# Delta-rule kernel: the 32x32 blocks and their inverses cross DRAM in quarters, one DMA each

## The chip, the cores and the metric

One core of a Trainium2 chip runs the whole kernel. The metric is the device time of one execution in microseconds (us); the median of the runs is compared.

## The reference, cut to what matters

The block takes x (4 x 256 x 256, float32), normalises it, and adds to x two branches: a gated delta-rule attention with 16 key heads and 32 value heads of width 128, and a mixture of 8 experts with a shared one. The change touches the attention branch only. Its core, per sequence and value head:

```python
def step(St, inp):
    q_t, k_t, v_t, g_t, b_t = inp
    St = St * jnp.exp(g_t)[..., None, None]
    v_old = jnp.einsum('bhk,bhkv->bhv', k_t, St)
    delta = (v_t - v_old) * b_t[..., None]
    St = St + k_t[..., None] * delta[:, :, None, :]
    o = jnp.einsum('bhk,bhkv->bhv', q_t, St)
    return (St, o)
```

The kernel doesn't scan. For a chunk of 128 tokens the recurrence is a triangular system: with N the decayed, negated products of the keys among themselves, the deltas are (I - N)^-1 applied to the values. So for every chunk a unit triangular 128x128 matrix is inverted.

## The kernel before, in words

A first stage (to about 240 us) does the norm, the routing and the experts. The change is in the second stage, a software pipeline over the 16 key heads; one pass of it is called a head here. Per head there are B x REP = 8 pairs of a sequence and a value head, and two chunks of 128 tokens each: NM = 16 matrices to invert.

**Making N.** ScalarE writes silu of the convolved k and q into kq (L1018). TensorE multiplies them in the items K0 to K3 (L1297, L1299), one for each sequence. VectorE scales the products by the decays into nm (L1160), 16 instructions a head, each adding 1 to nm_made. Of each nm row, w = 0 holds key with key and w = 1 key with query.

**Inverting.** Only the four 32x32 blocks on the diagonal of a matrix (the quarters q = 0 to 3) are inverted by elimination, on GpSimd. The SP queue moves them through DRAM, so that each of the 64 blocks has rows of its own on a partition:

- blocks_out (L878): SP waits for nm_made; for each q and chunk k one DMA writes 8 blocks to n_scratch (L885, 8 DMAs of 32 KB); then, with all landed, two DMAs read all blocks into halves[0] (L890). The upper 64 partitions work on the even rows of the inverses, the lower 64 on the odd ones.
- eliminate (L952): 31 steps of two instructions on GpSimd (L969, L972) and a turning copy (L975). Their semaphore is elim.
- blocks_back (L893): after the last step SP writes the inverse rows to r_scratch (L897, one DMA), and after the turning copy the turned ones to rt_scratch (L899, one DMA). With the latter landed it reads the turned blocks in six DMAs (L904: q = 0, 1, 2 by even and odd rows, semaphore turned_in) and the plain ones in eight into rf (L909: q = 0 to 3 by even and odd rows, into every second partition, semaphore back_in).

**Putting the inverse together.** TensorE and ScalarE do this in turns. LA1 (L1310) waits for all six turned transfers and multiplies blocks of N by turned inverses; ScalarE copies to p1 (L1062). LA2 (L1324) waits for all eight plain transfers. LB1 (L1337) and LB2 (L1345) do the same for the 64x64 blocks; then the values are solved (U1, N21, U2) and the outputs made (O).

**Order.** Each engine works through its own written list, ORDER for TensorE, ORDER_A for ScalarE, ORDER_V for VectorE, and waits at whatever item isn't ready. TensorE's has "... K2 OUT4 P7 P0 LA1 K3 LA2 P1 OUT5 LB1 OUT6 LB2 P2 U1_0 ...", ScalarE's "... Z3 LA1 S5 S6 E3 LA2 P7 P0 ...", VectorE's "... P6 D3 OUT4 K3 P7 ...". So K3, the last part of N for the next head, stands behind LA1 of this head on TensorE, and its decay factors (E3) behind LA1 on ScalarE. P and Z are projections (L1256 to L1258), OUT the output projection (L1395). SP's list for a head is: the weights, blocks_back of this head, blocks_out of the next one, its decays (L871), w_out (L876). GpSimd's is: the low part of the next projection weights (L949), then the elimination of the next head. P0 waits for that low part.

Of the kernel before, what the change touches and what calls it, by code (L numbers as in the profile page):

```python
# [20 lines left out]
F32 = mybir.dt.float32  # L21
# [3 lines left out]
ALU = mybir.AluOpType  # L25
ACT = mybir.ActivationFunctionType

P = 128
B, S, D = 4, 256, 256
# [29 lines left out]
def build(nc, x, w_heads, w_out, w_b, w_a, dt_bias, A_log, norm_w, router_w, w_up, w_down, out):  # L59

    n_dram = nc.dram_tensor("n_scratch", (4, 2, REP * B, C32, C32), F32).ap()
    r_dram = nc.dram_tensor("r_scratch", (2, 4, 2 * REP * B, C32 // 2, C32), F32).ap()
    rt_dram = nc.dram_tensor("rt_scratch", (2, 4, 2 * REP * B, C32, C32 // 2), F32).ap()
    eg_dram = nc.dram_tensor("eg_scratch", (HK, REP * B * EC), F32).ap()

    with ExitStack() as ctx:
        def sb(name, shape, dt=F32, where=ctx):
            return where.enter_context(nc.sbuf_tensor(name, shape, dt))
# [585 lines left out]
        with ExitStack() as c3:  # L654
# [18 lines left out]
            nm = [sb(f"nm{i}", [P, BH, 2, EC], F32, c3) for i in range(2)]  # L673
# [8 lines left out]
            t64 = halves[1][0:C64].rearrange("p (m t) -> p m t", t=C64)  # L682
# [4 lines left out]
            tc2 = p1  # L687
# [29 lines left out]
            back_in = sem("inverse_blocks_in", c3)  # L717
            rt_out = sem("turned_inverse_blocks_out", c3)
            turned_in = sem("turned_inverse_blocks_in", c3)
            a_full = sem("ra_full", c3)  # L720
# [142 lines left out]
            def _(sp):  # L863
# [14 lines left out]
                def blocks_out(n, par):  # L878

                    at_least(sp, nm_made, 16, n, 16)  # L880
                    for q in range(4):
                        first = C32 * q
                        cols = nm[par][first:first + C32].rearrange("p m w e -> p (m w e)").rearrange("p (m k s) -> p k m s", k=3, s=S)
                        for k in range(2):
                            sp.dma_start(n_dram[q, k].rearrange("m i x -> i m x"), cols[:, k, :, first:first + C32]  # L885
                                         ).then_inc(blocks_out_sem, 16)
                    at_least(sp, blocks_out_sem, 128, n, 128)
                    at_least(sp, rt_out, 16, n, 0)
                    for h in range(2):
                        sp.dma_start(halves[0][C64 * h:C64 * (h + 1)],  # L890
                                     n_dram.rearrange("q k m i x -> (q k m) (i x)")).then_inc(rb_in, 16)

                def blocks_back(n, it):  # L893
# [3 lines left out]
                    sp.dma_start(r_dram.rearrange("h q m i x -> (h q m) (i x)"), rows[:, 0:HR * C32]).then_inc(r_out, 16)  # L897
                    sp.wait_ge(elim, NELIM * n + NELIM)
                    sp.dma_start(rt_dram.rearrange("h q m c i -> (h q m) (c i)"), halves[0][:, 0:C32 * HR]).then_inc(rt_out, 16)  # L899
                    sp.wait_ge(rt_out, 16 * n + 16)  # L900
                    at_least(sp, a_full, 1, it.a_before("U2_1"), 0)
                    for q, tile, step in ((0, t64[0:C32], C32), (1, t64[C32:C64, :, HR:], C32), (2, tc2[C64:C64 + C32], HR)):
                        for h in range(2):
                            sp.dma_start(tile[:, :, h * step:h * step + HR], rt_dram[h, q].rearrange("m c i -> c m i")  # L904
                                         ).then_inc(turned_in, 16)
                    sp.wait_ge(r_out, 16 * n + 16)
                    for q in range(4):
                        for h in range(2):
                            sp.dma_start(rf[C32 * q + h:C32 * (q + 1):2, :, C32 * q:C32 * (q + 1)],  # L909
                                         r_dram[h, q].rearrange("m i x -> i m x")).then_inc(back_in, 16)  # L910
# [27 lines left out]
            def _(gp):  # L938
# [13 lines left out]
                def eliminate(n, it):  # L952
# [4 lines left out]
                    at_least(gp, r_out, 16, n, 0)  # L957
# [39 lines left out]
            def _(a):  # L997
# [15 lines left out]
                def silu(n, it, q):  # L1013
                    a.wait_ge(conv_step, 24 * n + 3 * (q + 1))
                    if q < 4:
                        blk, half = piece(q)
                        at_least(a, kk_full, B, n, 0)
                        a.activation(kq[:, 2 * half:2 * half + 2, blk, :], conv[q % 2][:], ACT.Silu).then_inc(silu_made, 1)  # L1018
# [12 lines left out]
                def run(it):  # L1031
                    b, odd, items = it.b, it.odd, it.items_a
                    n, par = b + 1, 1 - odd
                    for item in items:
# [29 lines left out]
                        elif item == "LA2":  # L1064
# [3 lines left out]
                            a.copy(t64[C32:C64].rearrange("p m (h j) -> p m h j", h=2)[:, :, :, 0:HR],  # L1068
                                   bank[C32:C64].rearrange("p m (i h) -> p m h i", h=2))
# [44 lines left out]
            def _(v):  # L1114
# [18 lines left out]
                def key_scales(n, it, par):  # L1133
# [5 lines left out]
                    v.tensor_scalar(sk[:].rearrange("p (b c) -> p b c", c=2), sums[:, :, 0, :], EPS_L2, None, ALU.add).then_inc(small, 1)  # L1139
                    v.tensor_scalar(sqe[par][:].rearrange("p (b c) -> p b c", c=2), sums[:, :, 1, :], EPS_L2, EPS_RMS * P,  # L1140
# [8 lines left out]
                def decayed(n, par, b_, it):  # L1149
# [5 lines left out]
                    for c, lo, hi, at in ((0, 0, S, P), (1, S, EC, 0)):  # L1155
                        w = hi - lo
                        bank = it.bank[f"K{b_}" + "ab"[c]][:, 0:2 * w].rearrange("p (w s) -> p w s", w=2)
                        for r in range(REP):
                            bh = b_ * REP + r
                            v.scalar_tensor_tensor(out=nm[par][:, bh, :, lo:hi], in0=bank, scalar=wneg[:, 2 * b_ + c, r:r + 1],  # L1160
# [75 lines left out]
            def _(te):  # L1236
# [36 lines left out]
                def across(par, m, first, size):  # L1273

                    at = S * (m // BH) + first + size
                    return nm[par][first:first + size, m % BH, 0, at:at + size]

                def run(it):
                    b, odd, items = it.b, it.odd, it.items_te
                    n, par = b + 1, 1 - odd  # L1280
                    for item in items:
# [11 lines left out]
                        elif k == "K":  # L1293
# [3 lines left out]
                            te.matmul(bank[:], kq[:, i, 0, 0:P], kq[:, i, :, :].rearrange("p w s -> p (w s)"), start=True, stop=True)  # L1297
                            bank = fill(it, f"K{i}b")
                            te.matmul(bank[:, 0:S].rearrange("p (w s) -> p w s", w=2), kq[:, i, 0, P:S], kq[:, i, :, P:S],  # L1299
# [10 lines left out]
                        elif item == "LA1":  # L1310
# [3 lines left out]
                            te.wait_ge(turned_in, 96 * b + 96)  # L1314
# [131 lines left out]
```

## Time and profile before

| | us |
|---|---|
| median of 3 runs | 1172.33 |
| lowest and highest | 1170.95, 1179.87 |
| the profiled execution, device time | 1175.13 |
| its span in the trace | 1173.2 |
| mean granted TensorE clock in it | 0.952 |

The span is the time from the first to the last instruction in the trace, 1.9 us less than the device time of the same execution. A view lists for each engine how long it was busy; the rows of the timeline give the start, the length, the line and the form of instructions, merged where they follow each other, and in square brackets how long the engine had been idle before and what ended it. SPq is the queue of SyncE; a row of it is the time in which it issued a DMA, not that in which the data moved.

### The profile page before, as it was taken

Reading aid. Unit: us, or ns where it says so; the run is one execution under the profiler, and the core shown is the slowest. Engines: PE = TensorE matmul, PEld = TensorE weight load, DVE = VectorE, ACT = ScalarE, POOL = GpSimd, SP = SyncE. Lnnn points to the kernel's source line nnn. Section 1 sums busy time; section 2 is a strip of 40 time slices with the busy share of each in tenths; the row PEclk is TensorE's granted clock in tenths of the full one; section 3 lists DMA queues with packets and bytes.
Section 4 is the critical chain, followed back from the end, with each engine's and each line's share of the span. In section 5 each row is a group of like instructions: output and inputs, shape, how many; then the busy total and the mean of one; then the engine's idle time right before and its main releaser. Section 6 shows DMA issues by size and latency. Waiting matters only on the chain.

```text
span 1173.2 us, 22375 instructions
## 1 busy us (share of the span) xinstructions
PE 1051.0 (90%) x8190; PEld 801.7 (68%) x8190; DVE 813.8 (69%) x1469; ACT 601.5 (51%) x1150; POOL 519.3 (44%) x1140
## 2 busy tenths in 40 slices
PE   3999999966689989998989889998999999988867
PEld 3786666645476767776777767676778777776756
DVE  4622222259849878897979887987888797968424
ACT  2521222234556747574746656574757474745523
POOL 2421000055745547283828364554728282835520
PEclk9999999988879999999989999998989898999979
DMA  9930110044131323324142413232332413231111
GB/s 331 365 124 19 45 46 28 23 157 127 29 115 36 117 45 109 69 84 115 57 100 59 128 31 121 38 115 44 109 69 83 115 56 98 61 102 33 39 35 45
DMA packets 155098, 103.18 MB, mean 88 GB/s; under 512 B 125168, under 2 KB 139120, under 8 KB 151664
## 3 DMA queue, kind: packets, MB, share of 16 engines
q1 hardware_dynamic: 153456, 97.56, 28.6%
q0 software_dynamic: 1536, 4.20, 1.1%
q8 instruction: 67, 1.10, 0.4%
q14 instruction: 39, 0.32, 0.1%
HBM read 79.77 MB, written 21.95 MB: 87 GB/s over the span
## 4 chain that ended last, share of the span: by engine, by line
PE 27%; POOL 20%; SPq 9%; DVE 8%; DMA 8%; issue 5%; ACT 2%; POOLq 0%; DVEq 0%; ACTq 0%
POOL rows L972 10%; POOL rows L969 9%; SPq L909 4%; PE pj L1256 3%; DVE nm L1160 3%; DMA halves<-n_scratch 3%; PE rg L1395 3%; PE pj L1257 3%; PE pj L1258 3%; SPq L885 3%; DVE conv L1122 3%; PE rg L1362 2%; PE rg L1378 2%; SPq L904 2%; DMA rf<-r_scratch 2%
## 5 line engine op out<-in xcount | busy, mean ns | idle before, releaser
L1122 DVE SCALAR_TENSOR_TENSOR conv<-pj,taps,conv 128x510 f32<-128x510 f32 (+2 forms) x384 | 283.9, 744 | 104.2 <-ACT conv L1010 94.6
L969 POOL TENSOR_TENSOR rows<-rows,halves 128x126 f32<-128x126 f32 (+22 forms) x496 | 187.8, 379 | 336.8 <-DMA halves<-n_scratch 299.2
L972 POOL TENSOR_TENSOR rows<-rows 128x126 f32<-128x126 f32 (+22 forms) x496 | 195.2, 393 | 38.9
L1256 PE MATMUL pj<-xhi,whi 128*128 128x512 f32 x384 | 182.0, 474 | 20.7 <-DVE conv L1122 13.5
L1257 PE MATMUL pj<-xlo,whi 128*128 128x512 f32 x384 | 159.1, 414 | 0.0
L1258 PE MATMUL pj<-xhi,wlo 128*128 128x512 f32 x384 | 158.9, 414 | 0.0
L1160 DVE SCALAR_TENSOR_TENSOR nm<-rg,wneg,eg 128x512 f32<-128x512 f32 (+1 forms) x256 | 138.1, 607 | 10.5 <-ACT eg L1053 6.6
L1395 PE MATMUL rg<-wo,gated 128*128 128x256 f32 x512 | 138.0, 402 | 0.1
L1256 PEld LDWEIGHTS pj<-xhi,whi 128*128 128x128 f32 x384 | 76.0, 198 | 53.4 <-issue 29.9
L1395 PEld LDWEIGHTS rg<-wo,gated 128*128 128x128 f32 x512 | 99.6, 200 | 18.1 <-issue 1.3
L1010 ACT ACTIVATE conv<-pj,taps 128x512 f32<-128x512 f32 x128 | 87.6, 694 | 46.3 <-PE pj L1258 42.9
L1131 DVE TENSOR_TENSOR_SCAN eg<-eg,start 128x256 f32<-128x256 f32 x128 | 94.0, 791 | 0.5
L1258 PEld LDWEIGHTS pj<-xhi,wlo 128*128 128x128 f32 x384 | 76.5, 199 | 18.6
L1257 PEld LDWEIGHTS pj<-xlo,whi 128*128 128x128 f32 x384 | 77.0, 201 | 13.0
L1226 DVE SCALAR_TENSOR_TENSOR acc<-rg,fr,acc 128x256 f32<-128x256 f32 x128 | 60.9, 476 | 29.5 <-PE rg L1395 29.0
L1378 PE MATMUL rg<-nm,zz 128*128 128x256 f32 x256 | 77.6, 385 | 1.9 <-ACT zz L1088 1.9
L1096 ACT ACTIVATE vn<-rg,ssk 128x128 f32<-128x128 f32 x256 | 73.1, 384 | 0.4 <-PE rg L1307 0.4
L1297 PE MATMUL rg<-kq 128*128 128x512 f32 x128 | 70.1, 630 | 0.0
L977 POOL MEMSET rf<- 128x2048 f32 x1 | 1.8, 1804 | 148.9 <-POOLq L200 148.9
L1204 DVE SCALAR_TENSOR_TENSOR gated<-rg,nwneg,zs 128x512 f32<-128x512 f32 x64 | 46.2, 746 | 30.7 <-ACT sq L1104 16.5
L1229 DVE SCALAR_TENSOR_TENSOR acc<-rg,fr,acc 128x256 f32<-128x256 f32 x128 | 61.9, 484 | 4.5
L1362 PEld LDWEIGHTS rg<-vn,rf 128*128 128x128 f32 x512 | 61.8, 192 | 3.9 <-ACT rf L1082 1.2
(197 smaller groups left out, 1948.3 us busy)
## 6 DMA issues: line engine op xcount, KB each, us to landing
eg<-eg_scratch SPq DMA_DIRECT2D x16, 1536.0 KB, 7.9
wraw<-w_heads SPq DMA_DIRECT2D x16, 776.0 KB, 4.6
w1a<-w_up SPq DMA_DIRECT2D x10, 1024.0 KB, 9.7
halves<-n_scratch SPq DMA_DIRECT2D x32, 256.0 KB, 3.8
w2a<-w_down SPq DMA_DIRECT2D x8, 512.0 KB, 12.5
wo<-w_out SPq DMA_DIRECT2D x16, 256.0 KB, 2.7
n_scratch<-nm SPq DMA_DIRECT2D x128, 32.0 KB, 1.7
r_scratch<-rows SPq DMA_DIRECT2D x16, 256.0 KB, 2.0
```

Source lines behind the costliest of these rows:

```text
L969: gp.tensor_tensor(tmp, rb[:, 0:r, t:t + 1].to_broadcast([P, r, w]), nb[:, t:t + 1, t + 1:].to_broadcast([P, r, w]), ALU.mult).then_inc(el ...
L972: gp.tensor_tensor(rb[:, 0:r, t + 1:], rb[:, 0:r, t + 1:], tmp, ALU.add).then_inc(elim, 1)
L1010: a.activation(conv[j % 2][:], it.pbank[item][:], ACT.Copy, scale=taps[par][:, piece(j)[0], KS - 1:KS]).then_inc(tap_made, 1)
L1122: v.scalar_tensor_tensor(out=y, in0=it.pbank[item][:, :, 0:S - s], scalar=taps[par][:, piece(j)[0], KS - 1 - s:KS - s], in1=y, op0=ALU.mul ...
L1131: v.tensor_tensor_scan(decay, decay, start[:, 0:S], 0.0, ALU.mult, ALU.add).then_inc(decay_made, 1)
L1160: v.scalar_tensor_tensor(out=nm[par][:, bh, :, lo:hi], in0=bank, scalar=wneg[:, 2 * b_ + c, r:r + 1], in1=eg[:, r, b_, at:at + w].unsqueez ...
L1256: te.matmul(bank, whi[par][w], xhi[:, k, cols], start=(k == 0), stop=False)
L1257: te.matmul(bank, whi[par][w], xlo[:, k, cols], start=False, stop=False)
L1258: ins = te.matmul(bank, wlo[par][w], xhi[:, k, cols], start=False, stop=(k == KD - 1))
L1362: ins = te.matmul(bank[:, q * P:(q + 1) * P], rf[:, m, :], vn[:, m, :], start=True, stop=True)
L1378: te.matmul(bank[:, r * S:(r + 1) * S], zz[:, s, :], nm[odd][:, s, 1, 0:S], start=True, stop=False)
L1395: ins = te.matmul(bank[:, r * D:(r + 1) * D], gated[:, r, t * P:(t + 1) * P], wo[:, r, :], start=True, stop=True)
```

## The change

N's layout and those of the three scratch tensors are changed so that a quarter q of all 16 matrices moves in one DMA.

- nm holds for each pair 768 columns: query-key of the first chunk row (0 to 255), key-key of it (NEAR = 256), query-key of the second chunk (SECOND = 512), key-key of it (FAR = 640). The diagonal blocks of all 16 matrices then lie 384 columns apart. To get this order kq holds q first and k second, and the matrices are numbered by pair and chunk (m = 2 * pair + chunk).
- n_scratch is written in 4 DMAs of 64 KB (8 of 32 KB before).
- r_scratch has rows in their natural order, so it is written in two DMAs, even rows and odd rows, each row of 128 bytes put 256 bytes behind the last (before: one DMA with 2 KB in one piece for each partition). rt_scratch is written in two DMAs, each partition's 2 KB still in one piece.
- The turned blocks are read in 3 DMAs (6 before), the plain ones in 4 (8 before), into all 32 partitions of a quarter.
- The order of reading is: turned 0, turned 2, plain 1, plain 3, turned 1, plain 2, plain 0. LA1 waits for the first two, LA2 for plain 1 and 3, LB1 for turned 1, LB2 for plain 2 and 0.
- The engines' lists are as they were. Matmuls, copies and VectorE instructions are the same in number and size; some read or write in another stride.

```diff
                     for q in range(4):
-                        first = C32 * q
-                        cols = nm[par][first:first + C32].rearrange("p m w e -> p (m w e)").rearrange("p (m k s) -> p k m s", k=3, s=S)
-                        for k in range(2):
-                            sp.dma_start(n_dram[q, k].rearrange("m i x -> i m x"), cols[:, k, :, first:first + C32]
-                                         ).then_inc(blocks_out_sem, 16)
-                    at_least(sp, blocks_out_sem, 128, n, 128)
-                    at_least(sp, rt_out, 16, n, 0)
+                        first = NEAR + C32 * q
+                        rows_of = nm[par][C32 * q:C32 * (q + 1)].rearrange("p b e -> p (b e)").rearrange("p (m s) -> p m s", s=EC)
+                        sp.dma_start(n_dram[q].rearrange("m i x -> i m x"), rows_of[:, :, first:first + C32]
+                                     ).then_inc(blocks_out_sem, 16)
+                    at_least(sp, blocks_out_sem, 64, n, 64)
+                    at_least(sp, rt_out, 32, n, 0)
...
                     sp.wait_ge(elim, NELIM * n + NELIM - 1)
-                    sp.dma_start(r_dram.rearrange("h q m i x -> (h q m) (i x)"), rows[:, 0:HR * C32]).then_inc(r_out, 16)
+                    for h in range(2):
+                        sp.dma_start(r_dram.rearrange("q m (i h) x -> h (q m) i x", h=2)[h],
+                                     rb[C64 * h:C64 * (h + 1)]).then_inc(r_out, 16)
                     sp.wait_ge(elim, NELIM * n + NELIM)
-                    sp.dma_start(rt_dram.rearrange("h q m c i -> (h q m) (c i)"), halves[0][:, 0:C32 * HR]).then_inc(rt_out, 16)
-                    sp.wait_ge(rt_out, 16 * n + 16)
+                    for h in range(2):
+                        sp.dma_start(rt_dram.rearrange("q h m c i -> h q m (c i)")[h],
+                                     halves[0][C64 * h:C64 * (h + 1), 0:C32 * HR]).then_inc(rt_out, 16)
+                    sp.wait_ge(rt_out, 32 * n + 32)
                     at_least(sp, a_full, 1, it.a_before("U2_1"), 0)
-                    for q, tile, step in ((0, t64[0:C32], C32), (1, t64[C32:C64, :, HR:], C32), (2, tc2[C64:C64 + C32], HR)):
-                        for h in range(2):
-                            sp.dma_start(tile[:, :, h * step:h * step + HR], rt_dram[h, q].rearrange("m c i -> c m i")
-                                         ).then_inc(turned_in, 16)
-                    sp.wait_ge(r_out, 16 * n + 16)
-                    for q in range(4):
-                        for h in range(2):
-                            sp.dma_start(rf[C32 * q + h:C32 * (q + 1):2, :, C32 * q:C32 * (q + 1)],
-                                         r_dram[h, q].rearrange("m i x -> i m x")).then_inc(back_in, 16)
+                    def turned_back(q, tile, landed):
+                        sp.dma_start(tile.rearrange("p h m i -> p (h m) i"), rt_dram[q].rearrange("h m c i -> c (h m) i")
+                                     ).then_inc(landed, 16)
+                    def rows_back(q, landed):
+                        sp.dma_start(rf[C32 * q:C32 * (q + 1), :, C32 * q:C32 * (q + 1)],
+                                     r_dram[q].rearrange("m i x -> i m x")).then_inc(landed, 16)
+                    turned_back(0, t64[0:C32, :, :, 0:HR], turned_in)
+                    turned_back(2, tc2, turned_in)
+                    sp.wait_ge(r_out, 32 * n + 32)
+                    rows_back(1, back_odd)
+                    rows_back(3, back_odd)
+                    turned_back(1, t64[C32:C64, :, :, HR:], turned_mid)
+                    rows_back(2, back_even)
+                    rows_back(0, back_even)
...
                         elif item == "LA1":
-                            te.wait_ge(turned_in, 96 * b + 96)
+                            te.wait_ge(turned_in, 32 * b + 32)
...
                         elif item == "LA2":
-                            te.wait_ge(back_in, 128 * b + 128)
+                            te.wait_ge(back_odd, 32 * b + 32)
...
                         elif item == "LB1":
+                            te.wait_ge(turned_mid, 16 * b + 16)
...
                         elif item == "LB2":
+                            te.wait_ge(back_even, 32 * b + 32)
```

## Rows read from the trace of the kernel before

**Rows 1.** the page, part 1: busy time, share of the span, instructions

```profile
PE 1051.0 (90%) x8190; PEld 801.7 (68%) x8190; DVE 813.8 (69%) x1469; ACT 601.5 (51%) x1150; POOL 519.3 (44%) x1140
```

**Rows 2.** PE waits, 420 to 1020 us: waiter, waited for, us, times, longest

```profile
PE rg L1330 <- DMA rf<-r_scratch: 26.3, 11, 3.4
PE rg L1319 <- issue: 6.0, 5, 1.3
```

**Rows 3.** stretches: length, busy us of each engine, PEclk, DMA share, GB/s

```profile
487.20:542.10 54.90, 49.38 (x456) 38.62 (x456) 46.81 (x82) 33.37 (x66) 29.49 (x68) 1.00 0.30 82
542.10:596.00 53.90, 50.70 (x456) 39.65 (x456) 44.45 (x78) 33.48 (x66) 29.62 (x68) 0.96 0.31 83
...
420.00:1020.00 600.00, 560.36 (x5013) 438.87 (x5012) 499.14 (x867) 364.50 (x722) 325.86 (x751) 0.96 0.30 82
```

**Rows 4.** timeline of the SP queue, first and last steady head, one head, tail

```profile
420.52 0.33 SPq L897 DMA_DIRECT2D r_scratch<-rows  x1
...
528.40 0.33 SPq L897 DMA_DIRECT2D r_scratch<-rows  x1
529.58 0.33 SPq L899 DMA_DIRECT2D rt_scratch<-halves  x1
531.60 1.91 SPq L904 DMA_DIRECT2D halves<-rt_scratch  x4
533.55 1.02 SPq L904 DMA_DIRECT2D p<-rt_scratch  x2
534.62 5.91 SPq L909 DMA_DIRECT2D rf<-r_scratch  x8
542.10 4.82 SPq L885 DMA_DIRECT2D n_scratch<-nm  x8
548.20 1.13 SPq L890 DMA_DIRECT2D halves<-n_scratch  x2
...
1019.65 0.33 SPq L897 DMA_DIRECT2D r_scratch<-rows  x1
...
1079.74 5.16 SPq L909 DMA_DIRECT2D rf<-r_scratch  x8
1084.94 5.00 SPq L885 DMA_DIRECT2D n_scratch<-nm  x8
```

**Rows 5.** timeline of PE: the first matmul of LA1 and of LA2

```profile
536.30 0.18 PE L1319 MATMUL rg<-halves,nm 32*32 32x32 f32 x1 [1.23 <-issue]
...
542.16 0.21 PE L1330 MATMUL rg<-rf,p 32*32 32x32 f32 x1 [3.17 <-DMA rf<-r_scratch]
...
1131.12 0.23 PE L1319 MATMUL rg<-halves,nm 32*32 32x32 f32 x1 [6.89 <-issue]
```

**Rows 6.** timeline of DVE: the last four nm instructions of two heads

```profile
539.88 2.19 DVE L1160 SCALAR_TENSOR_TENSOR nm<-rg,wneg,eg 128x512 f32<-128x512 f32 x4 [1.86 <-ACT eg L1053]
...
594.54 2.19 DVE L1160 SCALAR_TENSOR_TENSOR nm<-rg,wneg,eg 128x512 f32<-128x512 f32 x4
```

**Rows 7.** timeline of POOL: an elimination's first instruction, and the copy behind it

```profile
552.93 0.24 POOL L969 TENSOR_TENSOR rows<-rows,halves 128x31 f32<-128x31 f32 x1 [18.65 <-DMA halves<-n_scratch]
...
581.81 1.18 POOL L975 COPY halves<-rows 128x512 f32<-128x512 f32 x1
```

**Rows 8.** issues of SP by line: count, ns min/median/max, first and last start

```profile
L885 SPq DMA_DIRECT2D n_scratch<-nm x128: 308/451/1818, 273.4 to 1089.5; - x128
L904 SPq DMA_DIRECT2D halves<-rt_scratch x64: 303/488/1417, 316.3 to 1127.6; - x64
L909 SPq DMA_DIRECT2D rf<-r_scratch x128: 601/609/1952, 319.3 to 1134.9; - x128
L222 SPq DMA_DIRECT2D xs_scratch<-start x2: 641/6576/12510, 12.3 to 13.0; - x2
```

**Rows 9.** stretches, as rows 3: reading turned blocks, and writing n_scratch

```profile
642.00:644.00 2.00, 2.00 (x11) 1.66 (x10) 2.00 (x5) 0.00 (x0) 1.47 (x4) 1.00 0.66 62
275.00:277.00 2.00, 0.00 (x0) 0.00 (x0) 2.00 (x6) 0.00 (x0) 0.00 (x0) 1.00 0.44 66
```

More of the change, by code:

```diff
@@ L672, in build @@
             ssk = sb("ssk", [P, NT], F32, c3)
-            nm = [sb(f"nm{i}", [P, BH, 2, EC], F32, c3) for i in range(2)]
+            nm = [sb(f"nm{i}", [P, BH, 2 * EC], F32, c3) for i in range(2)]
+            NEAR, SECOND, FAR = S, 2 * S, 2 * S + P
             halves = [sb(f"halves{i}", [P, NM * C64], F32, c3) for i in range(2)]
@@ L681, in build @@
             prod = rows[:, HR * C32:]
-            t64 = halves[1][0:C64].rearrange("p (m t) -> p m t", t=C64)
+            t64 = halves[1][0:C64].rearrange("p (h m j) -> p h m j", h=2, j=C32)
             rf = sb("rf", [P, NM, P], F32, c3)
@@ L1017, in silu @@
                         at_least(a, kk_full, B, n, 0)
[L1018 removed]
+                        a.activation(kq[:, 2 * half:2 * half + 2, 1 - blk, :], conv[q % 2][:], ACT.Silu).then_inc(silu_made, 1)
                     else:
@@ L1273, in across @@
                 def across(par, m, first, size):
-                    at = S * (m // BH) + first + size
-                    return nm[par][first:first + size, m % BH, 0, at:at + size]
+                    at = (FAR if m % 2 else NEAR) + first + size
+                    return nm[par][first:first + size, m // 2, at:at + size]
                 def run(it):
@@ L1296, in run @@
                             bank = fill(it, f"K{i}a")
-                            te.matmul(bank[:], kq[:, i, 0, 0:P], kq[:, i, :, :].rearrange("p w s -> p (w s)"), start=True, stop=True)
+                            te.matmul(bank[:], kq[:, i, 1, 0:P], kq[:, i, :, :].rearrange("p w s -> p (w s)"), start=True, stop=True)
                             bank = fill(it, f"K{i}b")
-                            te.matmul(bank[:, 0:S].rearrange("p (w s) -> p w s", w=2), kq[:, i, 0, P:S], kq[:, i, :, P:S],
+                            te.matmul(bank[:, 0:S].rearrange("p (w s) -> p w s", w=2), kq[:, i, 1, P:S], kq[:, i, :, P:S],
                                       start=True, stop=True).then_inc(kk_full, 1)
@@ L1360, in run @@
                             for q in range(4):
-                                m = c * BH + 4 * i + q
-                                ins = te.matmul(bank[:, q * P:(q + 1) * P], rf[:, m, :], vn[:, m, :], start=True, stop=True)
+                                m = 4 * i + q
+                                ins = te.matmul(bank[:, q * P:(q + 1) * P], rf[:, 2 * m + c, :], vn[:, c * BH + m, :], start=True, stop=True)
                             ins.then_inc(a_full, 1)
@@ L1369, in run @@
                                 s = 4 * i + q
-                                ins = te.matmul(bank[:, q * P:(q + 1) * P], nm[odd][:, s, 0, P:S], zz[:, s, :], start=True, stop=True)
+                                ins = te.matmul(bank[:, q * P:(q + 1) * P], nm[odd][:, s, NEAR + P:NEAR + S], zz[:, s, :], start=True, stop=True)
                             ins.then_inc(v_full, 1)
@@ L1377, in run @@
                                 s = i * REP + r
-                                te.matmul(bank[:, r * S:(r + 1) * S], zz[:, s, :], nm[odd][:, s, 1, 0:S], start=True, stop=False)
-                                ins = te.matmul(bank[:, r * S + P:(r + 1) * S], zz[:, BH + s, :], nm[odd][:, s, 1, S:EC],
+                                te.matmul(bank[:, r * S:(r + 1) * S], zz[:, s, :], nm[odd][:, s, 0:S], start=True, stop=False)
+                                ins = te.matmul(bank[:, r * S + P:(r + 1) * S], zz[:, BH + s, :], nm[odd][:, s, SECOND:FAR],
                                                 start=False, stop=True)
```

35 lines of the change are left out of this document (17 added, 18 removed).

## The prediction

> **What bounds the kernel now.** I read the page's busy times first. TensorE is busy 90% of the span and no other engine over 69% [rows 1], but an average doesn't say what stands in its way, so next come the steady heads, those that begin with the write of the inverse rows at 420.52 and at 1019.65 us [rows 4]: 11 heads in 599.13 us, 54.47 us each. In that stretch TensorE is busy 560.36 of 600 us at a mean granted clock of 0.96 [rows 3], which is 50.9 us a head; 3.6 us a head it is idle. Its waits name the cause: 26.3 us in 11 waits of LA2 for the plain blocks, 6.0 us in 5 at LA1 [rows 2]. After such a wait the clock is low for a while: the head from one LA2 to the next with 49.38 us of work ran at clock 1.00; the next, with the same 456 matmuls, took 50.70 at 0.96 [rows 3]. So all in all the missing blocks cost TensorE 2.4 + 0.55 us of idle time and about 1.5 us of slow clock (50.9 - 49.4).
>
> Then the SP queue, to see why they are late. Call the issue of the inverse rows (528.40) t = 0. The turned ones go at 1.18, have landed at 3.20, their six reads are issued until 6.17, the eight plain ones until 12.13 [rows 4]. LA1 starts at 7.90, LA2 at 13.76 [rows 5]. VectorE makes the last nm at 11.48 to 13.67, after a wait for ScalarE, which stood at LA1 [rows 6]; SP sends N at 13.70, starts reading it at 19.80 [rows 4], GpSimd starts the next elimination at 24.53 and the next copy behind it is at 53.41 [rows 7]. That is a closed ring:
>
> 7.9 (to LA1) + 5.8 (LA1 to nm) + 6.1 (N out) + 4.7 (N in) + 28.9 (elimination) = 53.4 us.
>
> So two rings bind by turns: this one at 53.4, and TensorE's own list, 49.4 of work plus its stalls and its slow clock. The average of both is the 54.5 seen. The step from LA1 to nm is longer when VectorE is behind: at 594.54 it makes the last nm with no idle time before it [rows 6].
>
> **The change, part by part.**
>
> *N out: 8 DMAs to 4.* Issuing 8 took 4.82 us here and 5.00 at 1084.94 [rows 4]; at the least and the median of one issue, with the gap of 0.04 between two, it would be 0.31 + 7 x 0.49 = 3.7 [rows 8]. The last needs about 1.3 more to land (548.20 less the end of the issues, 546.92). Four take 0.31 + 3 x 0.49 = 1.8 us. Each has twice the packets: 512 of 128 bytes, 32 for each of 16 DMA engines. What one costs: in 275 to 277 us only such writes ran, 0.44 x 16 x 2 us for 66 GB/s x 2 us / 128 B = 1031 packets, 13.7 ns each [rows 9]; 16 more for each engine are 0.2 us. Sum 1.8 + 1.5 = 3.3; I take 3.7, since issues get held up now too (4.82 for 3.7). It saves 2.4 us.
>
> *Does the issue grow with the packets?* No row shows a DMA of 1024 short pieces issued alone. L904's have 512 and take 488 ns, L885's 256 and take 451; the fill of xs_scratch, 2944 pieces of 512 bytes, was issued in 641 (its second stood 12.5 us in a full queue) [rows 8]. Bounds: 0.45 us if it doesn't grow, 1 us if it does as the pieces. The 641 ns row is nearest: I take 0.5.
>
> *Inverse rows and turned rows out: 1 + 1 DMAs to 2 + 2.* The second turned write is issued 0.35 us later. Ahead of it in the same queues are now 2048 packets of 128 bytes, 128 an engine x 13.7 = 1.75 us, instead of 128 packets of 2 KB. They start at about 0.9 and end near 2.7, where the turned ones would have started at 2.1: 0.6 us late at most. Together I take 0.6 (bounds 0.35 and 1.0). Turned blocks landed at 3.8. The Trainium skill, "DMA: Bandwidth & Descriptors", Rules for kernel authors, says two transfers to disjoint halves of the partitions serialise; by that the split costs just its issue, and the sum would be 0.25 less.
>
> *Turned blocks in: LA1 waits for two DMAs, not six.* Issues 0.3 + 0.5, the second starting at 0.35. A read of 64-byte pieces costs an engine 10.9 ns each (0.66 x 16 x 2 us for 62 GB/s x 2 us / 64 B = 1938) [rows 9], so 64 pieces are 0.7 us where 32 were 0.35. Now the last of six is issued at 534.08 and LA1 starts 2.2 later; new: 0.35 + 2.2 + 0.35 + 0.2 behind the first = 3.1 after the landing, against 4.7 now. LA1 at 3.8 + 3.1 = 6.9, say 7.0: 0.9 saved. P0 ahead of LA1 ends at 6.7 (LA1's start less its 1.23 us of idle time [rows 5]), so nothing else holds it.
>
> *Plain blocks in: LA2 waits for two.* They are the third and fourth in the queue: landed at 3.8 + 0.35 + 3 x 0.55 + 2.5 = 8.3. LA2 needs ScalarE's copy of LA1 and comes behind K3; with K3 done at about 539 less 0.9, LA2 starts near t = 9.7 without a wait. The 2.4 us idle time of a head goes, and most of the slow clock with it. The new waits of LB1 and LB2 (behind them stand OUT6, P2, U1) are for the fifth to seventh DMA, landed by about 3.8 + 0.35 + 6 x 0.55 + 2.4 = 9.9; LB1 comes behind P1 and OUT5, ten large matmuls after LA2: nothing. If that cover were gone, each us late would be one of TensorE's idle time.
>
> *Free otherwise:* swapped kq, nm's order, matmul operands in two runs of 32 columns: same sizes. SP is free at about 7.7 instead of 12.1, long before nm at 12.8. It counts at the edges: at 1084.94 it sent N in the breath after its last plain read [rows 4].
>
> **The sum.** Ring through GpSimd: 7.0 + 5.8 + 3.7 + 4.7 + 28.9 = 50.1. TensorE: 49.4 + 0.3 for its copy waits = 49.7. Two rings so close, with VectorE at 45.4 us a head (499.14 / 11), disturb each other: I add 0.7, 50.8 us a head, 3.7 less than now. Over 16 heads 58.6 (the first and last have the same steps, and the last LA1 wait of 6.89 us [rows 5] shrinks by all that came before): span 1173.2 - 59 = 1114. The profiled execution took 1.9 more than its span, 1175.1, and the median 2.8 less than that. So the median comes to 1114 - 0.9, rounded to 1114.
>
> **The rivals.**
>
> 1. *VectorE takes over.* It has 45.4 us of work in 50.8, conv, nm and acc in a fixed list. Where it had no idle time before nm [rows 6], an earlier LA1 gains nothing, and TensorE then waits for its PSUM banks. Against it: over 600 us TensorE's two longest waits are for the blocks, not for VectorE [rows 2]. If LA1 to nm becomes 7.3, the ring is 51.6, and with the 0.7, 52.3: 16 x 2.2 = 35 less, 1137.
> 2. *The issue grows with the pieces.* 1 us each: N out stays 6.1, the two turned reads take 2, turned out is 0.7 later: ring 53.2, 16 x 1.3 = 20 less, 1152. The 641 ns row speaks against it [rows 8].
> 3. *The short writes block the queue: slower.* Inverse rows go as 128-byte pieces, interleaved by two DMAs. If one costs 4 x 13.7 = 55 ns, an engine has 7 us of them, the turned rows land at 9, LA1 comes 5.2 later than I say, ring 55.3: 16 x 0.8 = 13 more, 1185. It decides from about 48 ns a packet on. Against it: n_scratch's are of that size [rows 9]. The same page of the Trainium skill, Specifications, says writes under 512 bytes are read, changed and written back. n_scratch's 13.7 ns contain that already, so by the page too it is my figure; only two DMAs meeting in one 512-byte line is not in the trace.
> 4. *No change:* the idle time moves to LA1 and the clock stays low: TensorE 50.9 + 3. Against it: the ring itself is shorter by parts that are on it.
>
> **Chances.** My forecast (1100 to 1126) 0.60, rival 1 0.16, rival 2 0.12, rival 3 0.06, rival 4 0.06. A measurement can tell 1% from no change, 12 us. Faster: 0.60 + 0.16 + most of 0.12 = 0.87; within 1%: 0.07; slower: 0.06. Low end: both rings at 49.7 with a full clock, 16 x 4.7 = 75 less, 1098. High end: rivals 1 and 2 up to 1150.
>
> **What would show it.** Right: SP's four N issues in under 2.2 us; LA2 without a wait; LA1 about 7 us after the first inverse-row DMA; 50 to 51 us a head; clock nearly 1.00. Wrong: issues of 1 us; turned rows landing after t = 4.8; VectorE at the head of TensorE's waits; LA2 gone from the list but LA1 in its place with 3 us a head.

## The result, and the profile after

| | before | changed |
|---|---|---|
| median of 20 runs, us | 1178.31 | 1180.25 |
| lowest to highest, us | 1170.95 to 1180.90 | 1177.38 to 1185.78 |
| ratio, 95% interval | | 1.0033 (1.002 to 1.0046) |
| span of the profiled execution, us | 1173.2 | 1179.9 |
| mean granted TensorE clock in it | 0.952 | 0.941 |

The forecast was 1114, 5% faster. The change made the kernel slower by 0.3%, a difference that its interval sets apart from none. Repeated in a later group of runs (change_again) it gave 1.002 (0.9999 to 1.0041).

The page of the changed kernel, part 1 (engine, busy us, share, instructions): TensorE is as busy as before [rows 1].

```profile
PE 1057.2 (90%) x8190; PEld 803.7 (68%) x8190; DVE 813.7 (69%) x1469; ACT 601.1 (51%) x1150; POOL 519.2 (44%) x1140
```

The waits of TensorE in it from 420 to 1020 us (waiter, waited for, us, times, longest), to be read against [rows 2]. LA2, which had stood 26.3 us, is gone from the list. LA1 has 37.7 us instead of 6.0.

```profile
PE rg L1330 <- issue: 37.7, 11, 4.8
PE rg L1363 <- issue: 3.7, 11, 0.3
PE pj L1268 <- issue: 3.4, 5, 1.3
```

The SP queue of the changed kernel for one head, against [rows 4]:

```profile
525.57 1.27 SPq L900 DMA_DIRECT2D r_scratch<-rows  x2
526.89 1.48 SPq L904 DMA_DIRECT2D rt_scratch<-halves  x2
532.76 0.33 SPq L910 DMA_DIRECT2D halves<-rt_scratch  x1
533.14 0.56 SPq L910 DMA_DIRECT2D p<-rt_scratch  x1
533.75 1.34 SPq L914 DMA_DIRECT2D rf<-r_scratch  x2
535.15 0.48 SPq L910 DMA_DIRECT2D halves<-rt_scratch  x1
535.67 1.12 SPq L914 DMA_DIRECT2D rf<-r_scratch  x2
541.89 1.91 SPq L887 DMA_DIRECT2D n_scratch<-nm  x4
546.32 1.15 SPq L892 DMA_DIRECT2D halves<-n_scratch  x2
```

The reads are as quick as forecast, seven in 4.03 us where fourteen took 8.93. But the first of them starts at t = 532.76 - 525.57 = 7.19, and before it did at 3.20: what SP waits for there is that the two DMAs of turned rows land. The stretches of the changed kernel show how they go (length, busy us of PE, PEld, DVE, ACT, POOL, PEclk, DMA share, GB/s):

```profile
528.00:529.00 1.00, 1.00 (x6) 0.90 (x5) 0.62 (x3) 0.69 (x1) 1.00 (x1) 1.00 0.77 117
529.00:530.00 1.00, 1.00 (x6) 0.77 (x5) 0.96 (x2) 0.00 (x0) 1.00 (x1) 1.00 0.24 58
530.00:531.00 1.00, 1.00 (x4) 0.54 (x3) 0.96 (x2) 0.59 (x2) 1.00 (x1) 1.00 0.25 84
531.00:532.00 1.00, 1.00 (x6) 0.83 (x5) 0.96 (x3) 0.58 (x2) 0.88 (x3) 1.00 0.23 88
```

To 529 the inverse rows go in short packets with most engines busy. Then come three microseconds at a DMA share (the mean busy share of the 16 DMA engines) of 0.23 to 0.25 and 58 to 88 GB/s: four of 16 engines' worth. The same turned rows in the kernel before, one stretch:

```profile
530.50:531.00 0.50, 0.50 (x5) 0.42 (x4) 0.50 (x2) 0.00 (x0) 0.50 (x1) 1.00 1.00 389
```

All 16 engines and 389 GB/s. The DMA packets in the traces (a packet is one contiguous piece, here of 2 KB) split the delay. From SP's issue of the first turned write to its seeing them landed it is 2.04 us on average in the kernel before and 6.05 in the changed one. The first packet starts 0.85 us after that issue before, 1.87 now; from the first packet to the end of the last it takes 0.82 us before, 3.75 now. So about 1.0 us is the later start and 2.9 the slow transfer.

A late LA1 then costs more than its idle time. In the changed kernel LA1 starts at 591.41 after 4.78 us of idle time; behind it the granted clock is half, 1.2 instead of 2.4 GHz, K3 comes late, and VectorE waits 6.35 us for it before the last nm. The first matmul, the stretch behind it, and VectorE's row:

```profile
591.41 0.23 PE L1330 MATMUL rg<-halves,nm 32*32 32x32 f32 x1 [4.78 <-issue]
```

```profile
591.40:596.00 4.60, 4.59 (x68) 2.97 (x68) 0.00 (x0) 2.23 (x5) 0.00 (x0) 0.50 0.30 41
```

```profile
596.23 2.19 DVE L1172 SCALAR_TENSOR_TENSOR nm<-rg,wneg,eg 128x512 f32<-128x512 f32 x4 [6.35 <-PE rg L1311]
```

The steps of the ring, each the mean over the 11 steady heads, taken from the timelines of SP, PE and POOL, in us from the first inverse-row DMA (in kernels that issue the turned rows first, from the last elimination step):

| kernel | turned rows landed | LA1 | LA2 | N sent | N read | elimination | a head |
|---|---|---|---|---|---|---|---|
| before | 3.24 | 8.51 | 13.69 | 14.60 | 20.56 | 25.66 | 54.47 |
| changed | 7.37 | 10.76 | 14.84 | 17.33 | 21.53 | 26.48 | 55.34 |
| rt16 | 4.57 | 8.57 | 11.35 | 14.51 | 18.51 | 23.45 | 52.30 |
| rt16_first | 4.25 | 8.13 | 11.28 | 14.20 | 18.44 | 23.56 | 52.54 |
| b_rt8 | 5.31 | 9.99 | 15.68 | 16.08 | 22.01 | 27.28 | 56.10 |
| b_rt4 | 6.38 | 11.05 | 16.78 | 17.33 | 23.44 | 28.70 | 57.60 |
| rt16_long | 4.21 | 7.58 | 10.71 | 13.56 | 17.68 | 22.70 | 51.60 |
| rt16_first_long | 4.25 | 7.61 | 10.68 | 13.55 | 17.78 | 22.84 | 51.84 |
| rt16_n8 | 4.77 | 8.43 | 11.85 | 14.68 | 20.53 | 25.44 | 54.43 |
| b_order | 3.33 | 7.31 | 10.72 | 13.48 | 18.94 | 24.12 | 53.03 |
| n4_alone | 3.22 | 8.93 | 13.96 | 15.04 | 19.39 | 24.44 | 53.34 |
| order_n4 | 3.24 | 7.21 | 10.34 | 13.30 | 17.64 | 22.46 | 51.34 |
| order_n4_short | 3.21 | 14.22 | 16.84 | 20.53 | 24.63 | 29.62 | 49.41 |

In the changed kernel N takes 4.2 us from sending to reading where it took 6.0, a gain of 1.8. The turned rows land 4.1 later; LA1 waits for two reads and not for six and so follows them by 3.4 instead of 5.3, which leaves it 2.25 later. LA1 to nm takes 6.6 for 6.1. Sum: 2.25 + 0.5 - 1.8, so 0.9 us a head longer.

### The profile page after: what moved, and what is told of

Its sections match the earlier page's. It is cut to its first block, busy times and chain, and to the rows that moved or that the text cites. A ratio compares the mean times of both kernels' runs of the same rounds, so it can differ in the third digit from the quotient of the medians.

```text
span 1179.9 us, 22231 instructions
## 1 busy us (share of the span) xinstructions
PE 1057.2 (90%) x8190; PEld 803.7 (68%) x8190; DVE 813.7 (69%) x1469; ACT 601.1 (51%) x1150; POOL 519.2 (44%) x1140
## 4 chain that ended last, share of the span: by engine, by line
PE 64%; issue 6%; DVE 4%; POOL 2%; ACT 1%; DMA 1%; SPq 0%; ACTq 0%; DVEq 0%
PE rg L1408 9%; PE pj L1268 8%; PE pj L1269 7%; PE pj L1270 7%; PE rg L1309 5%; PE rg L1375 5%; PE rg L1391 5%; PE rg L1383 3%; PE rg L1392 2%; PE rg L1311 2%; PE rg L1319 2%; PE rg L1363 2%; PE rg L1354 2%; PE rg L1301 1%; PE rg L1341 1%
## 5 line engine op out<-in xcount | busy, mean ns | idle before, releaser
L1268 PE MATMUL pj<-xhi,whi 128*128 128x512 f32 x384 | 179.2, 467 | 19.3 <-DVE conv L1135 12.6
L1269 PE MATMUL pj<-xlo,whi 128*128 128x512 f32 x384 | 156.0, 406 | 0.0
L1270 PE MATMUL pj<-xhi,wlo 128*128 128x512 f32 x384 | 155.3, 405 | 0.0
L1268 PEld LDWEIGHTS pj<-xhi,whi 128*128 128x128 f32 x384 | 74.8, 195 | 53.6 <-issue 32.6
L1238 DVE SCALAR_TENSOR_TENSOR acc<-rg,fr,acc 128x256 f32<-128x256 f32 x128 | 60.9, 476 | 29.6 <-PE rg L1408 29.0
L1076 ACT COPY p<-rg 128x512 f32<-128x512 f32 x16 | 9.8, 612 | 139.4 <-PE rg L1332 139.4
L1309 PE MATMUL rg<-kq 128*128 128x512 f32 x128 | 78.9, 702 | 0.0
L1330 PE MATMUL rg<-halves,nm 32*32 32x32 f32 x512 | 24.9, 215 | 58.9 <-issue 48.9
L1330 PEld LDWEIGHTS rg<-halves,nm 32*32 32x32 f32 x512 | 23.3, 131 | 65.2 <-issue 64.3
```

What stands on the lines that cost most here:

```text
L1268: te.matmul(bank, whi[par][w], xhi[:, k, cols], start=(k == 0), stop=False)
L1269: te.matmul(bank, whi[par][w], xlo[:, k, cols], start=False, stop=False)
L1270: ins = te.matmul(bank, wlo[par][w], xhi[:, k, cols], start=False, stop=(k == KD - 1))
L1309: te.matmul(bank[:], kq[:, i, 1, 0:P], kq[:, i, :, :].rearrange("p w s -> p (w s)"), start=True, stop=True)
```

## The experiments

The level of the times differs between groups of runs: the kernel before had a median of 1188.6 us beside the first group (chip 0: rt16, rt16_first, b_rt4, b_rt8), 1189.9 beside the second (chip 4: rt16_long, rt16_first_long, rt16_n8, b_order) and 1179.7 beside the third (chip 4 again: order_n4, n4_alone, change_again, order_n4_short). Ratios are each to the kernel before in the same group. Two theories stood after the result. **Engines:** the turned rows are written by 4 of the 16 DMA engines, because the outermost dimension on the DRAM side, the quarters, has size 4 and doesn't merge with the matrices (the halves lie between them). **Short writes:** the 2048 packets of 128 bytes ahead of them hold the queue, rival 3 of the prediction.

### The layout of the turned rows: rt16

```diff
-    rt_dram = nc.dram_tensor("rt_scratch", (4, 2, 2 * REP * B, C32, C32 // 2), F32).ap()
+    rt_dram = nc.dram_tensor("rt_scratch", (4, 2 * REP * B, 2, C32, C32 // 2), F32).ap()
...
-                        sp.dma_start(rt_dram.rearrange("q h m c i -> h q m (c i)")[h],
+                        sp.dma_start(rt_dram.rearrange("q m h c i -> h (q m) (c i)")[h],
```

> The changed kernel with one edit: rt_scratch is laid out as quarter, matrix, half, so that the outermost dimension of each of its two writes is 64 (quarter and matrix merge) and no longer 4; the turned tiles have matrix before half to match. Engine theory (a DMA runs only on as many of the 16 DMA engines as divide the outermost dimension of both sides, so the changed kernel writes its turned rows on 4): the turned rows land 3.8 to 4.3 us after the first inverse-row DMA instead of 7.2, DMA share in that stretch goes from 0.24 to about 0.6, LA1's waits fall from 3.8 us to under 1 us each, and the time is 1120 (1105 to 1135). Short-write theory (the 2048 packets of 128 bytes ahead of them hold the queue): the landing stays within 0.5 us of 7.2 and the time within 6 us of the changed kernel's 1180.

Measured: ratio 0.9723 (0.9674 to 0.9771), 1154.31 us. Turned rows landed at 4.57, in the changed kernel 7.37. The stretch in rt16 in which they go:

```profile
535.50:536.50 1.00, 1.00 (x6) 0.88 (x5) 0.96 (x3) 0.01 (x1) 1.00 (x1) 1.00 0.73 256
```

The landing is just outside what I expected of the engines and 2.1 us below the least that the other theory allowed (6.7). In the packets, the transfer itself takes 1.0 us (3.75 in the changed kernel, 0.82 before); the late start, 1.89, is as it was. One transposition of two dimensions in a scratch tensor gives 3%. The time was worse than I expected: over 1172 us before, 1105 to 1135 is a ratio of 0.94 to 0.97, with 0.955 in the middle. So were LA1's waits, 16.7 us in 9 of them, where I expected each under 1 us.

### Short packets behind the turned rows: rt16_first

```diff
-                    sp.wait_ge(elim, NELIM * n + NELIM - 1)
-                    for h in range(2): ... r_dram ...
                     sp.wait_ge(elim, NELIM * n + NELIM)
                     for h in range(2): ... rt_dram ...
+                    for h in range(2): ... r_dram ...
```

> As rt16, and the two DMAs of inverse rows (the short packets) are issued behind the two of turned rows instead of ahead of them. Engine theory: the turned rows land at 3.4 to 3.6 us after the last elimination step, 0.3 to 0.7 us earlier than in rt16; that is at most 16 x 0.6 = 10 us less than rt16; plain rows land later, about 8 to 10 us after the step, which LA2 just hides. Short-write theory: this and not rt16 brings the landing down from 7.2, by about 3 us, so rt16 is near 1180 and this near 1130.

Measured: 0.966 (0.9629 to 0.969), 1148.01 us. The landing moved from 4.57 to 4.25, so the short packets had cost 0.3 us there, the low end of what I expected; that it would come at 3.4 to 3.6 was wrong. The interval overlaps that of rt16 and the means of a head don't order the two (52.30 and 52.54): a gain of a few us at most.

### Four and eight engines in the kernel before: b_rt4, b_rt8

The kernel before, with the same 2 KB pieces in the same partitions; only the size of the outermost dimension differs.

```diff
-    rt_dram = nc.dram_tensor("rt_scratch", (2, 4, 2 * REP * B, C32, C32 // 2), F32).ap()
+    rt_dram = nc.dram_tensor("rt_scratch", (2, 4, 2 * REP * B + 1, C32, C32 // 2), F32).ap()
...
-  sp.dma_start(rt_dram.rearrange("h q m c i -> (h q m) (c i)"), halves[0][:, 0:C32 * HR])
+  b_rt4, for each h:  sp.dma_start(rt_dram[h, :, 0:NM].rearrange("q m c i -> q m (c i)"), halves[0][C64 * h:C64 * (h + 1), 0:C32 * HR])
+  b_rt8:              sp.dma_start(rt_dram[:, :, 0:NM].rearrange("h q m c i -> (h q) m (c i)"), halves[0][:, 0:C32 * HR])
```

> The kernel before with one edit: rt_scratch has a 17th unused matrix in each quarter, so that quarter and matrix don't merge, and the turned rows are written in two DMAs with an outermost dimension of 4. Bytes and pieces (2 KB) are as before. Engine theory: each 128 KB go over 4 engines, 32 KB each at the 84 ns for 2 KB seen before, 1.35 us a DMA and 2.7 for both in place of 0.7: landing 2.3 us later (5.4 to 5.8 behind the last step, 3.2 before), ring longer by 2.3, time 1172 + 16 x 1.5 to 2.3 = 1196 to 1209. Short-write theory: there is no short write here, so nothing changes but one more issue, 1172 to 1178.

> As b_rt4, but the turned rows go in one DMA, whose outermost dimension is half and quarter merged, 8. Engine theory: 32 KB for each of 8 engines, 1.35 us in place of 0.7: landing 0.7 us later than before (3.9), time 1172 + 16 x 0.4 to 0.7 = 1178 to 1183. Short-write theory: as the kernel before, within 3 us.

Measured: b_rt4 1.0371 (1.0347 to 1.0396), landing 6.38; b_rt8 1.0188 (1.0158 to 1.0217), landing 5.31; before 3.24. The DMA shares are those of 4 and of 8 engines. A stretch of b_rt4, then one of b_rt8:

```profile
555.50:556.50 1.00, 1.00 (x7) 0.81 (x6) 1.00 (x3) 0.00 (x0) 1.00 (x1) 1.00 0.23 66
```

```profile
545.00:546.00 1.00, 1.00 (x6) 0.82 (x5) 0.96 (x2) 0.00 (x0) 1.00 (x1) 1.00 0.42 115
```

With no short write anywhere near, the fault of the changed kernel is made in the kernel before: in b_rt8 by a dimension alone, in b_rt4 by a dimension and a second DMA. The packets agree: when one of 2 KB starts, the median number under way is 16 in the kernel before, 9 in b_rt8, and 5 in b_rt4 and in the changed kernel. With rt16 that settles the cause. It is the rule of the Trainium skill, "DMA: Bandwidth & Descriptors", How many engines (k): a DMA runs on the largest number up to 16 that divides the outermost dimension of both sides. Shares of 0.23 for 4 of 16 and 0.42 for 8 of 16 agree. I had both sizes too small: with 8 engines the landing came 2.07 us later and not 0.7, with 4 in two DMAs 3.14 and not 2.3, and both times were above my ranges. At 115 GB/s in the stretch above each of eight engines moved 14 GB/s, while in the kernel before each of 16 had 24 (389 / 16). But that stretch is a mean over two phases. The whole transfer of b_rt8:

```profile
544.00:545.50 1.50, 1.50 (x9) 1.24 (x8) 1.12 (x3) 0.53 (x1) 1.50 (x1) 1.00 0.39 48
545.50:546.50 1.00, 1.00 (x5) 0.67 (x4) 0.96 (x2) 0.40 (x1) 1.00 (x1) 1.00 0.49 184
```

In its last microsecond the eight move 184 GB/s, 23 each, about what each of the 16 had. The time is lost before, where the same engines bring 48 GB/s. Why the transfer starts so slowly stays open.

### Long writes again: rt16_long, rt16_first_long

Inverse rows as in the kernel before, one DMA with 2 KB pieces, and so two reads for a quarter; in the second kernel that DMA goes behind the turned rows.

```diff
-                    for h in range(2): ... r_dram, 128-byte rows ...
+                    sp.dma_start(r_dram.rearrange("h q m i x -> (h q m) (i x)"), rows[:, 0:HR * C32]).then_inc(r_out, 16)
...
-                        sp.dma_start(rf[C32 * q:C32 * (q + 1), :, C32 * q:C32 * (q + 1)], r_dram[q] ...
+                        for h in range(2):
+                            sp.dma_start(rf[C32 * q + h:C32 * (q + 1):2, :, C32 * q:C32 * (q + 1)], r_dram[h, q] ...
```

> rt16 with the inverse rows as in the kernel before: written in one DMA, 2 KB in one piece for each partition, and so read in eight DMAs into every second partition (order plain 1, 3, 2, 0 as in the changed kernel). Theory that the short writes are dear: the 2048 packets of 128 bytes and their second issue hold the turned rows back by 0.8 us (they land at 4.57 on average in rt16, 3.24 in the kernel before); here they land at 3.7 to 3.9, LA1 comes 0.7 us earlier, and the time is 8 to 13 us under rt16. Theory that they cost nothing and only the fewer plain reads count: four more issues of 0.6 us, 0 to 5 us over rt16.

> rt16_long with the inverse rows' DMA issued behind the turned rows' two. If the short writes were the only thing that hurt ahead of the turned rows, this is within 4 us of rt16_long. If any write there costs (one issue of 0.33 us and 0.7 us of packets), the turned rows land 0.2 to 0.5 us earlier than in rt16_long and the time is 3 to 8 us less; LA2 still finds its blocks.

Measured: 0.9617 (0.9562 to 0.9672) and 0.9646 (0.9593 to 0.97). With the long writes LA1 comes at 7.58 instead of 8.57, and the kernel is 1% under rt16, though in another group of runs and with intervals that all but touch. By LA1's step, writing in the natural order to save four reads was a loss; in the time it is hardly shown, and against rt16_first (0.966) not at all. Once the writes are long it doesn't matter which write goes first. The landing stays at 4.2, 1.0 over the kernel before, which was more than I expected of rt16_long. What is left of the difference to the kernel before is that the turned rows go in two DMAs. The issues of SP by line, count, ns min/median/max, in rt16_long:

```profile
L902 SPq DMA_DIRECT2D rt_scratch<-halves x32: 470/536/1612, 324.9 to 1093.6; - x32
```

In order_n4 below, which writes them in one:

```profile
L901 SPq DMA_DIRECT2D rt_scratch<-halves x16: 319/326/607, 313.2 to 1077.7; - x16
```

Two issues of 0.54 against one of 0.33 are 0.75 us more of SP's own time. How much of the 1.0 us that makes is not shown, since the first half moves while the second is issued. In the packets the first one starts 1.13 us after the issue for 0.85, and the transfer takes 1.50 us for 0.82; a packet takes 140 ns on average for 84, which no run here explains.

### N in eight DMAs again: rt16_n8

```diff
-                        sp.dma_start(n_dram[q].rearrange("m i x -> i m x"), rows_of[:, :, first:first + C32]
+                        for k in range(0, NM, BH):
+                            sp.dma_start(n_dram[q, k:k + BH].rearrange("m i x -> i m x"), rows_of[:, k:k + BH, first:first + C32]
```

> rt16 with N sent in 8 DMAs of 32 KB again (each quarter in two halves of 8 matrices), in the new layout. Theory that N's way out is on the ring: from nm to the start of the read it takes 6.0 us again and not 4.0, the ring and a head are 1.5 to 2 us longer, 24 to 32 us over rt16. Theory that TensorE's own list binds by now and the saving is in its shadow: within 8 us of rt16.

Measured: 0.9889 (0.9826 to 0.9951). N needs 5.85 us from sending to reading (20.53 - 14.68), 4.0 in rt16, and a head 54.43 for 52.30. Against rt16 the ratio is 1.7% higher, about 20 us, a little less than the 24 to 32 expected. Of the whole change this is the part that works as forecast.

### Only the order: b_order

The kernel before, all DMAs as they were, but read as turned 0, turned 2 | plain 1, plain 3 | turned 1 | plain 2, plain 0, with the waits of LA1, LA2, LB1 and LB2 to match.

```diff
-                            te.wait_ge(turned_in, 96 * b + 96)
+                            te.wait_ge(turned_in, 64 * b + 64)
...
-                            te.wait_ge(back_in, 128 * b + 128)
+                            te.wait_ge(back_in, 64 * b + 64)
```

> The kernel before with nothing but the order and the waits of the reads as in the change: layouts, sizes and numbers of all DMAs as before; turned 0 and 2 first (four DMAs, LA1 waits for these), plain 1 and 3 (four, LA2), turned 1 (two, LB1), plain 2 and 0 (four, LB2). Theory that most of the gain is LA2's and LA1's earlier data: LA1 at 6.9 to 7.5 (8.51 before), LA2 without a wait, a head 52.9 to 53.3 us (54.47 before), ratio 0.976 to 0.985. Theory that one DMA for a quarter is what gains: ratio 0.99 to 1.00, LA1's waits grow as LA2's go.

Measured: 0.9862 (0.9795 to 0.9929). LA1 at 7.31 and LA2 at 10.72, nearly without a wait, and a head of 53.03, all as the first theory had it; the ratio is just outside its 0.976 to 0.985. LA1 is earlier here than in rt16_long, where it waits for half as many DMAs. The waits of TensorE from 420 to 1020 us in b_order show where the idle time went:

```profile
PE pj L1268 <- issue: 20.2, 11, 2.8
PE rg L1364 <- issue: 3.7, 11, 0.3
PE rg L1331 <- issue: 3.1, 6, 1.1
PE rg L1342 <- DMA rf<-r_scratch: 1.8, 4, 0.7
```

L1268 is P0, which stands ahead of LA1 and waits for the weights' low part; GpSimd makes that only when the elimination is over. In the head that begins at 535.07 it has made it at 539.97, P0 starts at 540.08 and LA1 at 542.09. TensorE comes there early now.

### N alone, both together, the change again: n4_alone, order_n4, change_again

n4_alone is the kernel before with nm's new layout and N in four DMAs. order_n4 adds b_order's reads and waits to it. change_again is the changed kernel once more.

```diff
# order_n4 against rt16_long
-    rt_dram = nc.dram_tensor("rt_scratch", (4, 2 * REP * B, 2, C32, C32 // 2), F32).ap()
+    rt_dram = nc.dram_tensor("rt_scratch", (2, 4, 2 * REP * B, C32, C32 // 2), F32).ap()
...
-                    for h in range(2): ... rt_dram.rearrange("q m h c i -> h (q m) (c i)")[h] ...
+                    sp.dma_start(rt_dram.rearrange("h q m c i -> (h q m) (c i)"), halves[0][:, 0:C32 * HR]).then_inc(rt_out, 16)
...
-                        sp.dma_start(tile.rearrange("p m h i -> p (m h) i"), rt_dram[q].rearrange("m h c i -> c (m h) i") ...
+                        for h in range(2):
+                            sp.dma_start(tile[:, :, h], rt_dram[h, q].rearrange("m c i -> c m i")).then_inc(landed, 16)
```

> The change's order of reads and waits and its N in four DMAs, with everything else as before: turned rows written in one DMA and read in two for a quarter, inverse rows written in one in pieces of 2 KB and read in two for a quarter. Adding up the steps measured so far: turned rows landed at 3.3, LA1 at 7.3 (as in the kernel with only the new order), N sent at 13.5, read from 17.6 (4.0 to 4.1 later, as in rt16_long), elimination from 22.6: a head 51.2 to 51.6 us, at or up to 8 us under rt16_long; ratio to before 0.955 to 0.965. If merging the reads of a quarter were itself a gain, this would be 5 us or more over rt16_long.

> The kernel before with only N in four DMAs (and the layout of nm that this needs); reads, their order and their waits as before. Theory of the two rings: the ring through GpSimd loses 2 us, but LA2 still waits for all plain blocks and TensorE keeps its idle time and its slow clock behind it (2.4 and about 1.5 us), so that its own list binds: a head 53.2 to 53.8 us, ratio 0.985 to 0.993. Theory that only the ring counts: 52.5, ratio 0.975.

> The changed kernel as it is, beside the others on their chip. Ratio to before 1.000 to 1.006 if its result doesn't hang on the chip; turned rows landing at 7.3 to 7.4.

Measured: order_n4 0.9582 (0.9555 to 0.9609), 1129.25 us where the kernel before had 1179.67, the lowest ratio of the complete kernels (its interval overlaps that of rt16_long), and a head of 51.34, as added up beforehand. n4_alone 0.9824 (0.9786 to 0.9862), a head of 53.34 as the theory of the two rings had it, the ratio a little better than its 0.985. change_again 1.002 (0.9999 to 1.0041), with the landing at 7.44. Each part alone gives 1.4 and 1.8%; together 4.2. With only one of the two rings shortened the other one holds: in n4_alone LA2 still waits 24.2 us for plain blocks, in b_order the ring through GpSimd keeps its slow way out for N (5.5 us). The waits and the stretch of order_n4:

```profile
PE rg L1327 <- issue: 7.0, 8, 3.7
PE pj L1265 <- issue: 5.6, 7, 1.5
PE rg L1338 <- DMA rf<-r_scratch: 5.3, 6, 1.1
PE rg L1360 <- issue: 3.7, 11, 0.3
```

```profile
420.00:1020.00 600.00, 575.13 (x5393) 451.40 (x5392) 529.93 (x915) 392.10 (x777) 342.80 (x792) 0.99 0.32 87
```

These four are 22 us, all its waits together 25, and the clock is at 0.99 where it was 0.96 [rows 3].

### The next bound: order_n4_short

```diff
-            NELIM = 2 * (C32 - 1) + 4
+            NELIM = 2 * 20 + 4
...
-                    for t in range(C32 - 1):
+                    for t in range(20):
```

> order_n4 with the elimination cut to its first 20 of 31 steps, so that the inverses are incomplete: about 9 us of GpSimd's work and of the ring are left out, and nothing else. If TensorE's own list is the next bound and costs 49.7 us a head as I worked out, a head takes 49.7 to 50.3 us and no longer follows the ring (which would be about 42). If VectorE takes over, TensorE's waits name it and a head takes over 50.5.

Measured: 0.9179 (0.9146 to 0.9211); a head 49.41. TensorE no longer waits for blocks at all. Its waits and its stretch:

```profile
PE rg L1360 <- issue: 3.3, 10, 0.3
PE rg L1298 <- ACT sqk L1058: 3.0, 1, 3.0
PE pj L1265 <- DVE conv L1132: 2.4, 1, 2.4
```

```profile
420.00:1020.00 600.00, 590.61 (x5465) 465.29 (x5462) 547.12 (x948) 398.84 (x788) 269.78 (x572) 0.99 0.33 89
```

TensorE is busy 98% of the time, VectorE 91% and not in its way. The floor of 49.7 worked out in the prediction was right within 0.3 us, and rival 1 was rightly put aside: even at this pace TensorE waits once for VectorE, 2.4 us.

## Why the prediction was wrong, point by point

- **What bounds the kernel: right in kind.** The two rings, and the price of the idle time in clock. n4_alone, b_order and order_n4 show both rings by turns, and order_n4_short TensorE's. But the steps that add up to 53.4 were read from one head, and a short one. The means in the table give 8.5 + 6.1 + 6.0 + 5.1 + 28.9 = 54.6 for the kernel before, the whole 54.47. TensorE's own list shows in the first of them: in six of 11 heads LA1 found its blocks there and came late for another reason.
- **"Inverse rows and turned rows out: 1 + 1 DMAs to 2 + 2": this step failed.** I took 0.6 us, bounds 0.35 and 1.0. It was 4.13 (7.37 - 3.24). The term left out is the number of engines. I divided the bytes of each write by 16 engines without looking at its shape; with the outermost dimension at 4 it is 32 KB for each of 4 engines and DMA. Going to 16 engines takes 2.8 us off (rt16), long writes 0.36 more (rt16_long), and the last 1.0 goes with the cut of the write in two. I had also priced the second issue at 0.35 us; in the changed kernel one issue of L904 takes 0.7.
- **N out: right**, but 0.5 low: 4.2 for 3.7 (4.0 in rt16); rt16_n8 shows it by itself.
- **LA2 without a wait: right.** Its 26.3 us are gone. The time of that idle wait turned up at LA1, in full (6.0 to 37.7 us), and with it the slow clock.
- **LA1 behind the landing: a bit low.** 3.1 forecast; 3.4 in the changed kernel and in rt16_long, 4.0 in rt16, where LA1 in two of 11 heads came later than its blocks. The second of the two reads of 64 KB lands 2.9 us after its issue (the median; 3.2 in rt16) where I had 2.4. With four of 32 KB LA1 comes 4.0 behind (b_order, order_n4), but there too some heads don't wait for the blocks. So merging the reads saves 0.6 us at most, and the split write that it needs costs 1.0.
- **Issues don't grow with the packets: right** for the reads and N (0.49 for 512 packets [rows 8], 0.56 for 1024 in the changed kernel); rival 2 fell. For the two writes cut in two it was not: an issue of inverse rows takes 0.62 and one of turned rows 0.7 us, where the uncut ones took 0.33.
- **Rival 3** named the right place (the landing of the turned rows) and the wrong cause. The short writes cost 0.3 to 0.4 us there, not 5. By the prediction's own ring a landing at 7.37 for 3.8 would be 50.1 + 3.6 = 53.7 us and still a gain; that the head took 55.34 shows that the ring's other steps were low too. Rivals 2 and 3 also leave out the 0.7 us that the forecast and rival 1 add, and rival 2's ring leaves out its slow reads. Rival 4, no change because the idle time moves to LA1, is nearest to what happened.
- **The chances: wrong.** All the faster cases shared one term, the write, and its bounds came from packets only. 0.13 for everything from no change down was too little for a kernel with four new access shapes.

The head was forecast at 50.8 and took 55.34. Of these 4.5 us the landing is 3.6; LA1 to nm is 0.8 (6.6 for 5.8), N out 0.5, N in and LA1 behind the landing 0.2 each, together 5.3, less the 0.7 that the forecast had added for rings that disturb each other. With 16 engines the forecast would still have been too low by 16 x 1.5 = 24 us: rt16 takes 52.30 us a head, not 50.8. Of this 0.8 is the landing and most of the rest LA1 behind it.

## What to carry to other kernels

When a scratch layout is changed so that a read becomes one DMA, look at what it does to the write, and at the outermost dimension of both sides after merging: 4 there meant 4 engines here, and 8 meant 8. The DMA share of the stretch shows it at a glance, here 0.23 to 0.25 for 4. Where two rings bind by turns, shorten both before judging either; alone, each part here gave under half of what they gave together. And when a wait goes from the list, ask which item of the same chain waits next: here it was LA1 in LA2's place. Reordering the reads (LA1's first, then LA2's) needed no new layout and gave 1.4% alone, where N in four DMAs gave 1.8%, with intervals that overlap.

## What the runs showed of the hardware that was not expected

A DMA of 256 KB on 8 engines took 4.11 us from issue to landing where that on 16 took 2.04. At full pace an engine was no slower (23 GB/s in the last microsecond, 24 on 16 in the best half microsecond), but ahead of that lay 1.5 us at 48 GB/s for all eight. Its issue took 642 ns where that on 16 took 326, with the same bytes and pieces. The line of b_rt8:

```profile
L899 SPq DMA_DIRECT2D rt_scratch<-halves x16: 638/642/705, 320.3 to 1156.6; - x16
```
